# A 16-batch transformer block on one core: the first experts' weights are issued behind the keys' transfers, A's packs a unit later, and the launch waits for less

## What is computed

```python
x = L0_attn_x                                  # (16, 512, 128)
xn = layernorm(x)
x = x + gqa(xn) + ffn0(xn)                     # gqa: 16 query heads, 4 key/value heads, "A" below
xn = layernorm(x)
x = x + mqa(xn) + swiglu(xn)                   # mqa: 16 query heads, 1 key/value head, "B" below

def ffn0(x):
    x = x + mla_attention(rmsnorm(x))          # latent keys and values, rope, causal, 16 heads: "M" below
    return x + moe(rmsnorm(x))                 # top 1 of 4 experts, 128 -> 512 -> 128, relu
```

## Time and profile before

| | |
|---|---|
| median of 3 runs | 3009.22 us (2998.30 to 3010.39) |
| profiled execution | 3022.93 us, of which the span 3021.2 us |
| PE busy | 2691.6 us, 89% |
| DVE busy | 2349.8 us, 78% |
| ACT busy | 1736.0 us, 57% |
| POOL busy | 1018.5 us, 34% |
| mean granted TensorE clock | 0.932 |
| DMA queue of SyncE | 175.12 MB, 19.2% of 16 engines |

### The profile page before, as it was taken

One profiled execution on the slowest core, in us unless ns is written; L12 is line 12 of the kernel. 1 busy time (PEld: TensorE's weight loads), 2 busy tenths in 40 slices (PEclk: granted clock), 3 DMA queues, 4 the chain that ended last, 5 costly groups with the idle time before them and its releaser, 6 DMA issues.

```text
span 3021.2 us, 114225 instructions
## 1 busy us (share of the span) xinstructions
PE 2691.6 (89%) x47344; PEld 1435.9 (48%) x47344; DVE 2349.8 (78%) x6003; ACT 1736.0 (57%) x3521; POOL 1018.5 (34%) x2006
## 2 busy tenths in 40 slices
PE   4869899999989989899998999999899899989968
PEld 1344454545445454454545445454454545445432
DVE  4768789787887969788786887978788787888825
ACT  1725656566565656656565565665656565565734
POOL 4233333333433323333233433323333233333110
PEclk7979999999999999999899999999899999999987
DMA  2031221303121130222203121130222203121120
GB/s 91 6 121 29 87 60 46 96 23 110 44 81 54 37 114 26 87 62 68 72 23 112 42 81 54 38 114 25 87 62 66 74 23 121 34 83 59 39 68 5
DMA packets 168021, 190.82 MB, mean 63 GB/s; under 512 B 24614, under 2 KB 150736, under 8 KB 167504
## 3 DMA queue, kind: packets, MB, share of 16 engines
q1 hardware_dynamic: 163408, 175.12, 19.2%
q0 software_dynamic: 4096, 8.40, 0.9%
HBM read 84.18 MB, written 16.25 MB: 33 GB/s over the span
## 4 chain that ended last, share of the span: by engine, by line
PE 69%; DVE 13%; issue 7%; POOL 4%; DMA 3%; ACT 2%; SPq 1%; ACTq 0%; DVEq 0%; POOLq 0%
PE bank L614 47%; PE pv L732 17%; DVE mx L959 7%; DMA wxs<-wx 2%; PE bank L620 2%; POOL moe L1400 2%; PE bank L742 2%; ACT probs L1197 1%; POOL probs L1350 1%; DVE xn L854 1%; DVE bank L964 1%; DVE bn L839 1%; SPq L583 1%; PE bank L784 1%; DVE factored L854 0%
## 5 line engine op out<-in xcount | busy, mean ns | idle before, releaser
L1197 ACT ACTIVATE probs<-bank 128x512 f32<-128x512 f32 x2688 | 1469.8, 598 | 950.4 <-PE bank L614 933.4
L959 DVE TENSOR_REDUCE mx<-bank 128x1 f32<-128x512 f32 x2048 | 1291.1, 681 | 104.6 <-PE bank L614 93.9
L964 DVE CUSTOM_DVE_ANT_0 bank<-bank,mask 128x128 f32<-128x128 f32 (+3 forms) x1024 | 484.7, 513 | 241.7 <-PE bank L614 238.3
L614 PE MATMUL bank<-kp_B,qp_B 72*32 72x512 bf16 x4096 | 443.3, 393 | 28.9 <-DVE mx L959 24.4
L1350 POOL TENSOR_SCALAR_AFFINE_SELECT probs<-probs 128x256 f32<-128x256 f32 (+1 forms) x640 | 231.8, 366 | 685.2 <-ACT probs L1197 676.3
L614 PE MATMUL bank<-kp_M,qp_M 72*32 72x128 bf16 (+3 forms) x4096 | 342.4, 322 | 116.1 <-issue 83.8
L614 PE MATMUL bank<-kp_A,qp_A 72*32 72x512 bf16 x4096 | 417.7, 407 | 24.8 <-DVE mx L959 22.4
L614 PE MATMUL bank<-qp_B,kp_B 74*32 74x512 bf16 x4096 | 435.6, 404 | 1.7 <-DMA qp_B<-nmT 1.2
L614 PE MATMUL bank<-qp_A,kp_A 74*32 74x512 bf16 x4096 | 412.1, 382 | 0.5 <-ACT probs L1197 0.5
L732 PE MATMUL pv<-probs,vv_B 128*32 128x512 f32 x2048 | 298.4, 638 | 5.0 <-ACT probs L1197 4.9
L614 PE MATMUL bank<-qp_M,kp_M 74*32 74x384 bf16 (+3 forms) x4096 | 286.8, 317 | 17.2 <-DVE mx L959 16.6
(11 more groups left out here) (162 smaller groups left out, 3247.3 us busy)
## 6 DMA issues: line engine op xcount, KB each, us to landing
wxs<-wx SPq DMA_DIRECT2D x112, 578.0 KB, 4.9
qp_M<-parts_q SPq DMA_DIRECT2D x144, 128.0 KB
kp_M<-parts_k SPq DMA_DIRECT2D x144, 128.0 KB
qp_A<-parts_q SPq DMA_DIRECT2D x144, 128.0 KB
qp_B<-parts_q SPq DMA_DIRECT2D x144, 128.0 KB
xp<-xq SPq DMA_DIRECT2D x16, 448.0 KB, 7.1
kp_A<-parts_k SPq DMA_DIRECT2D x144, 32.0 KB
xs<-x SPq DMA_DIRECT2D x16, 256.0 KB, 2.9
```

The lines of the kernel that those rows point to most:

```text
L614: ins = pe.matmul(dst[at:at + n], lhsT[:, at:at + n], rhs, start=start, stop=stop, tile_position=(0, at))
L959: v.tensor_reduce(mx[:, g % 2, at:at + 1], s1[BANK[a, g, u]][:], AX.X, ALU.max) \
L964: v.tensor_tensor_reduce(bank[:, 0:keys], bank[:, 0:keys], mask[:, SEQ - keys:SEQ], 1.0, LOWEST, ALU.add, ALU.max, mx[:, g % 2, at:at + 1] ...
L1197: act.activation(probs[:, slot, :], s2[BANK2[a, g, u]][:], ACT.Exp).then_inc(sig[f"{a}_exp"], 1)
```

## The change

- The plan's times move. The first three weights go from 3.32, 3.34 and 3.36 to 3.75, 4.15 and 4.55, behind all nine packs of M's keys; xp_in goes from 4.258 to 3.972 and stands between weights 0 and 1.
- A's packs stand one unit later (`pack_a`): the query's from 5.087, the keys' from 6.049 to 6.529, between weights 3 to 6. B's fourth shift rows are now ahead of all of them.
- The wait for the route is dropped for tiles 3 to 6.
- moe_added goes from 8.715 to 8.497 and the steps of B behind it come earlier with it (x1_norm 8.835 to 8.617, b_q 9.635 to 9.418); xp_turn goes from 5.105 to 5.269, up from 5.500 to 5.449, the last gather from 8.104 to 8.053, m_k from 2.727 to 2.655, A's and B's probs_v 0.027 later. Others shift by less.
- At launch x is the first transfer; VectorE waits for the weights only after the statistics of x; POOL fills the value tiles behind its first x_norm and signals them apart; ScalarE runs one Exp on a small tile first, so that its table is loaded.

```diff
-T = dict(x_load=-0.9, x_norm=-0.011, res0=1.0, x_scaled=0.46, turn_xr=0.9, m_q=1.107, split_mq=1.25, m_lat=0.98,
-         m_lat_turn=1.55, m_k=1.727, split_mk=1.85, m_v=1.95, turn_xn=2.262, a_q=2.542, split_aq=2.687, a_k=2.8,
-         a_v=3.432, split_ak=3.523, pack=0.4,
-         nms=1.15, nmT=1.5, lag=1.986, pv_M=3.37, pv=2.826, out_copy=1.188, out_turn=0.183, o_turn=0.145, o_proj=0.382,
-         x2_norm=0.352, e0=13.6, x2_scaled=-0.691, turn_r2=-0.5, gate=-0.318, ranks=0.157, route=0.15, route_step=0.044, scatter=0.75, xp_in=1.658, xp_turn=2.505, weights=0.724, up=2.9, step=0.246, later=0.3,
-         y_out=0.25, gather=0.618, moe_added=1.439, down=0.03,
+T = dict(x_load=-0.9, x_norm=-0.066, res0=1.148, x_scaled=0.46, turn_xr=0.9, m_q=1.107, split_mq=1.25, m_lat=0.995,
+         m_lat_turn=1.55, m_k=1.655, split_mk=1.85, m_v=1.95, turn_xn=2.309, a_q=2.542, split_aq=2.687, a_k=2.8,
+         a_v=3.432, split_ak=3.649, pack=0.4, pack_a=1.4,
+         nms=1.15, nmT=1.5, lag=1.986, pv_M=3.37, pv=3.265, out_copy=1.188, out_turn=0.125, o_turn=0.209, o_proj=0.382,
+         x2_norm=0.352, e0=13.6, x2_scaled=-0.691, turn_r2=-0.5, gate=-0.318, ranks=0.157, route=0.15, route_step=0.043, scatter=0.75, xp_in=1.372, xp_turn=2.669, weights=1.15, wgap=0.2, wnext=0.2, up=2.849, step=0.246, later=0.3,
+         y_out=0.25, gather=0.618, moe_added=1.272, down=0.03,
...
 LATE = {
-    "SP": dict(shift_turn=0.03),
+    "SP": dict(shift_turn=0.067),
...
-            put(t + T["pack"] + 0.06 * r, "pack", s, r)
+            put(t + T["pack_a" if s[0] == "a" else "pack"] + 0.06 * r, "pack", s, r)
...
         if j < WSLOTS:
-            put(e0 + T["weights"] + 0.02 * j, "weights", j)
+            put(e0 + T["weights"] + T["wgap"] * 2 * j, "weights", j)
...
+            sp.dma_start(xs[:], x[0].rearrange("(t p) d -> p t d", p=P)).then_inc(sig["x_loaded"], 16)
             for dst, src in ((w, w_all), (wl, w_lat), (vec, v_all), (rot, rope)):
...
                 slot = j % WSLOTS
-                sp.wait_ge(sig["route"], total(b, "route", TILE_EXPERTS))
+                if j < WSLOTS:
+                    sp.wait_ge(sig["route"], total(b, "route", TILE_EXPERTS))
...
             v.memset(half_neg[:], -0.5).then_inc(setup_dve, 1)
-            v.wait_ge(ld_w, 16 * 5)
-            v.wait_ge(setup_pool, 1)
...
                 stats(b, xs, bn[:, 0], mv[:, 0], "x_bn", "x_stats")
+                if b.first:
+                    v.wait_ge(ld_w, 16 * 5)
+                    v.wait_ge(setup_pool, 1)
...
+            act.wait_ge(setup_dve, 1)
+            act.activation(table_loaded[:], half_neg[:], ACT.Exp)
             act.wait_ge(ld_w, 16 * 5)
...
-            for a in "MBA":
-                link(pool.memset(vv[a][:], 0.0))
-                for h in range(VHEADS[a]):
-                    one = VHALF * (h // (GROUP if a == "M" else 1) % 2) + HD
-                    link(pool.memset(vv[a][:, :, h, one:one + 1], 1.0))
             pool.wait_ge(setup_dve, 1)
-            pool.wait_ge(ld_w, 16 * 5)
             pool.memset(seen[:], 0.0).then_inc(setup_pool, 1)
+
+            def values_setup():
+
+                for a in "MBA":
+                    link(pool.memset(vv[a][:], 0.0))
+                    for h in range(VHEADS[a]):
+                        one = VHALF * (h // (GROUP if a == "M" else 1) % 2) + HD
+                        link(pool.memset(vv[a][:, :, h, one:one + 1], 1.0))
+                pool.memset(seen[:], 0.0).then_inc(setup_pool, 1)
+                pool.wait_ge(ld_w, 16 * 5)
...
                 pool.tensor_scalar(sq[:, 6, :], sq[:, 5, :], 1.0, 0.0, ALU.mult, ALU.add).then_inc(sig["x_rstd"], 1)
+                if b.first:
+                    values_setup()
```

More of the change, by code:

```diff
@@ L115 @@
             "B": ((0, 4), (4, 8), (8, 12), (12, 16))}
[L119 to L125 removed]
+T = dict(x_load=-0.9, x_norm=-0.066, res0=1.148, x_scaled=0.46, turn_xr=0.9, m_q=1.107, split_mq=1.25, m_lat=0.995,
[4 more added lines that the diff above has]
+         y_out=0.25, gather=0.618, moe_added=1.272, down=0.03,
+         b0=0.12, x1_scaled=0.121, res1=0.75, turn_x1=0.513, b_q=0.801, split_bq=0.1, b_k=1.0, split_bk=0.228, b_v=1.248,
@@ L126 @@
          ff=1, ff_down=0.505)
 LATE = {
-    "SP": dict(shift_turn=0.03),
+    "SP": dict(shift_turn=0.067),
     "PE": dict(),
-    "DVE": dict(o_proj=0.024, x1_scaled=0.0, m_lat_turn=0.0, x_scaled=-0.056, m_lat=0.0, x1_norm=0.0, x2_norm=0.0,
+    "DVE": dict(o_proj=0.024, x1_scaled=0.022, m_lat_turn=0.0, x_scaled=-0.121, m_lat=0.0, x1_norm=0.0, x2_norm=0.0,
                 down=0.0, out_turn=0.0, gate=0.0),
-    "ACT": dict(turn=0.0, out_copy=0.0, o_turn=0.0, x_scaled=0.0, x2_scaled=0.0, shift_turn=0.017, m_v=0.0, up=-0.01),
@@ L134 @@
-    "POOL": dict(x_norm=0.106, x1_norm=0.184, x2_norm=0.042, m_lat=0.1, gate=0.1, m_q=0.023, m_k=0.05,
+    "ACT": dict(turn=0.0, out_copy=-0.063, o_turn=0.0, x_scaled=0.0, x2_scaled=0.0, shift_turn=0.017, m_v=0.0, up=-0.013),
+    "POOL": dict(x_norm=0.106, x1_norm=0.184, x2_norm=0.042, m_lat=0.1, gate=0.1, m_q=0.134, m_k=0.05,
                  split=0.0, score_exp=0.0),
@@ L198, in stages @@
         if j < WSLOTS:
-            put(e0 + T["weights"] + 0.02 * j, "weights", j)
+            put(e0 + T["weights"] + T["wgap"] * 2 * j, "weights", j)
         if j + WSLOTS < MOE_TILES:
-            put(t + T["later"] + 0.2, "weights", j + WSLOTS)
+            put(t + T["later"] + T["wnext"], "weights", j + WSLOTS)
     t += T["later"]
@@ L286, in kernel_program @@
         half_neg = sb("half_neg", [P, TILES])
+        table_loaded = sb("table_loaded", [P, TILES])
         xs = sb("xs", [P, TILES, D])
@@ L549, in x_load @@
             def x_load(b):
[L551 to L554, removed]
+                if b.first:
+                    return load_rest()
+                sp.wait_ge(sig["xn_ready"], total(b.prev, "xn_ready"))
+                sp.wait_ge(sig["res0_ready"], total(b.prev, "res0_ready"))
                 sp.dma_start(xs[:], batch(x, b)).then_inc(sig["x_loaded"], 16)
-                if b.first:
-                    load_rest()
             def shift_turn(b, a, g):
@@ L938, in value @@
                 v.wait_ge(sig[ps], total(b, ps, 3))
-                if not b.first:
+                if b.first:
+                    v.wait_ge(setup_pool, 2)
+                else:
                     v.wait_ge(sig[f"{a}_pv"], total(b.prev, f"{a}_pv"))
@@ L1171, in m_v @@
             def m_v(b):
+                if b.first:
+                    act.wait_ge(setup_pool, 2)
                 act.wait_ge(sig["mv_ps"], total(b, "mv_ps"))
```

## The result

| | before | after |
|---|---|---|
| median | 3009.8 us (4 runs, 2998.3 to 3013.5) | 2869.3 us (4 runs, 2862.0 to 2870.9) |
| ratio | 1 | 0.9535 [0.9504, 0.9565] |
| profiled execution, span | 3022.9, 3021.2 us | 2862.0, 2860.3 us |
| PE busy, mean clock | 2691.6 us, 0.932 | 2632.3 us, 0.960 |

The ratios leave out executions more than 1.5% above the fastest of the same kernel, so that of filled_short isn't that of its plain median.

A forecast was written before the change was run, and what follows sets the result against it. TensorE was taken to stand idle at M's first scores, its keys queued behind weights, then run at half clock. 77 + 54 + 8 + 7 - 5 - 9 = 132 us off 3022.9, less 13.7, gives 2877; range 2820 to 2950.

The forecast's parts named there:

- two-fold cost: At M's first scores, the late keys cost twice: TensorE's idle wait and a half-rate clock in the 11 us from M's start.
- M's wait, batches 2 to 15: Before M's first scores, keys ahead of weights cut 83.8 us of idle time to 7: gain 77 us (49 to 84).
- clock behind it: In the 11 us from M's first score, the half-rate stretch goes with the wait: gain 54 of 59 us, bound below 28.
- batch 1: At M's start in batch 1, undisturbed keys land at 180.8: 8.2 us gained, 8.2 us of wait left.
- launch: At the start, x first, fewer waits for VectorE and an early table load: gain 5.9 to 7.9 us, taken as 7.
- experts' weights: A's packs among weights 3 to 6 just fit; 0.3 us x 15 = 5 us charged (0 to 15).
- MoE's sum earlier: At moe_added, 2.5 us less distance to the gathers against 1.9 us of slack: 9 us of VectorE wait (0 to 20).
- small moves: A's and B's probs_v, out_turn, o_turn, m_k shift by one instruction: each between -5 and +5 us, taken as 0.
- M's keys: On SyncE's queue, reordered keys land at 532.2, just when TensorE is ready; 0.5 us of wait left per batch.
- Rival C: B's fourth shift rows wait behind weights and xp, the clock falls again: near no change (3018) 0.05, slower (3060) 0.05.
- Rival A: B's shift rows hold M's last three keys, 2.5 us wait per batch, clock falls in half: 78 us gain, 2931; chance 0.20.
- Rival B: VectorE's 63.7 us of waits and the second slow stretch also shrink: 2845, or 2820 with both; chance 0.10.

The follow-up runs named there:

- filled_short: Kernel before, with 5 groups of extra float32 matmuls run by TensorE before it waits for M's keys in batches 2 to 15: 0.9945 of before.
- filled_wait: Kernel before, with 11 groups of extra float32 matmuls run by TensorE before it waits for M's keys in batches 2 to 15: 3027.1 us, 1.0044.
- old_plan: Kernel after, with the plan's small moves undone; weights, xp_in, A's packs, SyncE's shift rows and launch stay changed: 2886.2 us, 0.9597 of before.
- packs_alone: Kernel before, with only A's packs one unit later; the weights stay between M's keys: 3030.2 us, 1.0048 of before.
- weights_and_packs: Kernel before, with the first three weights behind M's keys and A's packs one unit later: 2913.9 us, 0.9679 of before.
- weights_back: Kernel after, with the first three weights moved back between the second and third pack of M's keys: 2988.3 us, 0.9927 of before, 1.041 of after.
- weights_alone: Kernel before, with only the first three weights issued behind all packs of M's keys: 3003.7 us, 0.9968 of before.
- one_ahead: Kernel after, with the first of three weight transfers back between the second and third pack of M's keys: 2891.8 us, 0.9606 of before.
- wslots4_before: Kernel before, with four slots for the experts' weights instead of three, the fourth tile's weights issued behind A's query packs: 2986.5 us, 0.9897 of before.
- x_late: Kernel after, with x of the first batch loaded behind the weights again: 2870.7 us, 0.9540 of before.

## Why the prediction was right, and which terms were off

2877 us were predicted, 2869 measured, and 132 us of gain against 140.5. The place, the mechanism and the two-fold cost were right. The sum came out well partly by luck, because errors cancel:

| term | predicted | measured | from |
|---|---|---|---|
| M's wait, batches 2 to 15 | 77 | 83 | idle time without releaser 83.8 to 1.1 us |
| clock behind it | 54 | about 36 | filled_wait, 2.6 us a period |
| batch 1 | 8 | 5.5 | wait 16.36 to 10.89 us |
| launch | 7 | 8.2 | first matmul 20.84 to 12.62 us |
| experts' weights | -5 | -25 | waits 13.0 to 37.8 us |
| MoE's sum earlier | -9 | 0 | VectorE's wait for the gather 9.1 to 9.7 us |
| small moves | 0 | about 17 | old_plan, its share of the weights' waits within |

The measured terms add up to about 125 us, but they overlap. The last is net of the 18 us of weights' waits that the fifth counts too; with these back the sum is 143 us. It also holds some 5 us of M's wait (28.2 to 23.5 us). So I hold them to the right size, not to the last ten microseconds.

*M's keys.* The chain (copy, two shift issues, three key issues, 2.97 us to landing) gave 532.2 against a TensorE ready at 532.2, and I took 0.5 us of wait. In after, 508.93 + 3.1 = 512.04 with 0.18 us. That m_k stands earlier isn't what saved it: old_plan has it back in its old place and waits 0.1 to 0.5 us in these batches. In batch 1 the step that failed is the landing: 4.4 us from the end of the last issue to the first score, not 2.97.

*The clock.* The stretch at half rate is as read, and all of it went. But I took 54 of 59 us of missing full-rate time as lost, because VectorE was busy about half the time there or less. Two steps failed. The windows of the earlier trace rows begin 1 to 2 us before M's first score (356 against 357.01), and so count a part of the wait, when TensorE had nothing to do; windows that begin with the first score itself miss 50 us. And "the lost time is real" holds for a part only: filling the wait shows 36 us. The pair packs_alone and weights_and_packs, which differ by the weights' move alone, agrees: 111 us less by the ratios, of which 75.5 are idle time before M's first scores, which leaves 35 us for the clock and all else; its second part alone is 3.6 us shorter, 50 us over 14. So 36 us is the best figure, and up to 50 aren't excluded. That the rest is made up behind the stretch by the other engines' slack is my reading, not shown by a run.

*The experts' weights.* I costed the packs among the weights at 5 us and found that three or four of them just fit. packs_alone and weights_and_packs show 7 and 13 us for them, within the bounds. In packs_alone they put off weights 4 and 5 by 0.4 and 1.1 us. The larger part, 18 us, came with the small moves, which I had put at nothing: weights 6 stand behind M's second shift rows and go out 3.45 us after the slot is free, 1.24 before. That TensorE arrives sooner isn't the main cause: weights_back has 42.4 us with the old wait at M's start, and packs_alone and weights_and_packs, with and without that wait, have 19.9 and 23.2. Four slots save 59 us, more than any other cost that a run shows in after.

*MoE's end.* The failed step is the slack of 1.9 us. I counted the 2.6 us to the landing from the end of the last gather's issue, but they run from its start: in batch 3 it is issued at 774.73, landed at 777.25, and the add began at 780.21, 3.0 us later. In after the last gather starts 3.1 to 3.9 us before the add in 14 of 15 batches instead of 5.5 and more, so some 2 us are gone of the 2.5 planned, and it lands 0.0 to 2.3 us before the add. VectorE waits at most 0.3 us for it, but for the last batch, where the wait of some 9 us is the same in both kernels. The 9 us of cost came out as nothing, but the slack is nearly used up.

*The small moves.* I took 0, and old_plan shows about 17 us net: a shorter second slow stretch and a sooner start of M, less the waits for weights. Why the second stretch is shorter isn't shown.

*Rival C* was right in its mechanism and wrong in its condition. In weights_alone B's fourth shift rows did hold TensorE, 68.8 us in all, and the clock fell there, but only with A's query packs ahead of them, which the change had moved away: with weights and xp alone ahead (weights_and_packs), no score of B waits for them. *Rival A*, the edge, didn't happen, but by the rows of after an M start 1 us earlier would have met it (an estimate). *Rival B* happened in part: TensorE's waits for VectorE's maxima went from 63.7 to 44.1 us, and the second slow stretch from 64 to 44 us of missing full-rate time.

## What to carry to other kernels

In a queue served in order, look at what the small transfer that someone waits for stands behind, and after moving a large one, at who stands behind it now: here the keys and the shift rows both had to be cleared, and each edit alone was worth nothing. For a buffer that is refilled, measure from its release to the issue of the refill, and look at what the issuing engine has in its order between the two; a transfer that itself waits for something is the dear one. A buffer more can be worth more than the waits that the profile lists for it (59 us against 37.8). And don't book the missing full-rate time of a slow stretch in full: here 50 us of it cost some 36.

## What the runs showed of the hardware

- Idle waits before M's first scores, and the clock in the 11 us behind them: up to 1.30 us, 1.00 in all; from 1.36 to 2.22 us, below 1.00 behind three of six (0.84, 0.69, 0.69; one_ahead and filled_short); from 2.61 us up, below 1.00 behind every one (before, packs_alone, weights_back, wslots4_before, filled_short). With the wait filled by matmuls (filled_wait) it stayed at 1.00.
- In before the slow stretch missed 3.6 us of full-rate time a period behind M's first score (50 us over 14), and filling the wait gave back 2.6 us of time.
- A float32 matmul group of 4 x 512 columns took 0.85 us at full clock (11 groups in 9.4 us), twice what I had read off one instruction's row.
- The same 256 KB transfer of x landed by 3.8 us when issued first (0.80), and 7.3 us after its issue (3.14) when five transfers stood before it (x_late). In before, with the same five ahead but the next transfers issued later, it took 5.6 us (3.15 to 8.79).
